# Graph stage: routing, ranks and scatters of a group one step later, the first gather directly behind the second sum

## The reference

```python
mask_punct = (punct_graph == 1) & (aug_adj != 1)      # both are adj here: always empty
mask_aug = aug_adj == 1
deg = jnp.maximum(masks.sum(axis=2), 1.0)[..., None]
def conv(x, w_rel, w_root, b):
    out = x @ w_root + b
    out = out + (masks^T @ x / deg) @ w_rel            # for each mask
h = elu(conv(layernorm(x), w_rel1, w_root1, b1))
x = x + elu(conv(h, w_rel2, w_root2, b2))
```

```python
z = layernorm(x)
rw = softmax(z @ Wr); topw, topi = top_k(rw, 2); topw = topw / sum(topw)
shared = gelu(z @ W1s + b1s) @ W2s + b2s
```

## Time and profile before

| what | value |
|---|---|
| median of 3 runs | 2830.13 us (2828.23 to 2833.62) |
| profiled execution, its own time | 2831.41 us |
| its span | 2829.7 us |
| PE busy | 2695.7 us (95%) |
| VectorE busy | 1966.7 us (70%) |
| ScalarE busy | 1461.8 us (52%) |
| GpSimd busy | 1503.5 us (53%) |

### The profile page before, as it was taken

How to read it: one execution, slowest core, us unless ns; L and a number is a source line. 1 busy time by engine, 2 the same in 40 slices (tenths; PEclk the granted TensorE clock), 3 DMA queues, 4 the chain that set the end, 5 groups by cost and what they waited for, 6 DMA issues and landing times. The chain is left out here.

```text
span 2829.7 us, 87893 instructions
## 1 busy us (share of the span) xinstructions
PE 2695.7 (95%) x28783; PEld 2136.2 (75%) x28784; DVE 1966.7 (70%) x6881; ACT 1461.8 (52%) x2930; POOL 1503.5 (53%) x2542
## 2 busy tenths in 40 slices
PE   8999999899989999999999989999998999999999
PEld 4666666599957777777777767777778999999988
DVE  5666666577778888888888858788874454545453
ACT  3444444455546666666666535455554444444444
POOL 5555555333234444444444427777761666666674
PEclk8999999999989999999999999999999999999999
DMA  1111111000000000000000011111232222222264
GB/s 52 30 37 30 36 31 46 3 0 0 0 1 0 0 0 0 0 0 0 0 0 0 1 35 58 57 56 56 85 115 61 75 76 81 75 80 77 71 195 147
DMA packets 158090, 118.01 MB, mean 42 GB/s; under 512 B 20150, under 2 KB 145593, under 8 KB 158010
## 3 DMA queue, kind: packets, MB, share of 16 engines
q1 hardware_dynamic: 140602, 81.02, 10.4%
q0 software_dynamic: 17408, 35.95, 3.8%
HBM read 68.36 MB, written 48.56 MB: 41 GB/s over the span
## 5 line engine op out<-in xcount | busy, mean ns | idle before, releaser
L2025 POOL DMA_INDIRECT token_y<-e_y,e_rows x288 | 294.7, 1023 | 78.8 <-issue 73.1
L2068 ACT ACTIVATE e_hidden<-e_ps,e_b1g 128x512 f32<-128x512 f32 x288 | 194.6, 688 | 258.4 <-PE e_ps L90 257.8
L833 POOL TENSOR_TENSOR s_sw<-s_expo,s_rsum 128x512 f32<-128x512 f32 x128 | 133.5, 1043 | 355.4 <-DVE s_rsum L1094 355.4
L1301 POOL DMA_INDIRECT sorted_z<-r_z,r_rows x256 | 264.8, 1034 | 66.6 <-issue 61.8
L2120 PE MATMUL e_ps<-expert_w,e_hidden 128*128 x2304 | 280.3, 275 | 0.0
L460 DVE TENSOR_REDUCE a_V<-a_ps_s 128x8 f32<-128x1024 f32 x128 | 156.9, 1226 | 176.8 <-PE a_ps_s L399 176.8
L2120 PEld LDWEIGHTS e_ps<-expert_w,e_hidden 128*128 128x128 f32 x2304 | 273.9, 192 | 6.3
L324 ACT ACTIVATE a_probT<-a_ps_st 128x1024 f32<-128x1024 f32 x128 | 131.2, 1025 | 203.3 <-PE a_ps_st L407 203.3
L399 PEld LDWEIGHTS a_ps_s<-a_nT 16*128 16x128 f32 x2048 | 136.2, 188 | 91.5 <-issue 55.6
L2197 DVE TENSOR_TENSOR e_biased<-e_ps,expert_b 128x512 f32<-128x512 f32 x72 | 49.8, 691 | 213.8 <-PE e_ps L2120 213.8
L399 PE MATMUL a_ps_s<-a_nT 16*128 16x128 f32 x2048 | 185.6, 299 | 11.1
(11 more groups left out here) (400 smaller groups left out, 8033.8 us busy)
## 6 DMA issues: line engine op xcount, KB each, us to landing
e_z<-sorted_z SPq DMA_DIRECT2D x72, 260.0 KB
c_y<-token_y SPq DMA_DIRECT2D x22, 512.0 KB, 4.1
X<-in_x_dram SPq DMA_DIRECT2D x32, 256.0 KB, 2.8
a_adj<-in_adj_dram SPq DMA_DIRECT2D x32, 256.0 KB, 2.8
g_adj<-in_adj_dram SPq DMA_DIRECT2D x32, 256.0 KB
out_dram<-X SPq DMA_DIRECT2D x32, 256.0 KB, 2.6
c_y_s<-token_y SPq DMA_DIRECT2D x10, 512.0 KB, 5.0
token_y<-e_y,e_rows POOLq DMA_INDIRECT x288
```

Of the source, the lines that this page charges most:

```text
L833: nc.gpsimd.tensor_tensor(sw[p][:, :, :], expo[p][:, :, :], rsum[p][:, 1, :].unsqueeze(2).to_broadcast([T, HEADS, C]), ALU.mult).then_inc( ...
L1301: nc.gpsimd.indirect_dma_start(sh.sorted_z, bass.IndirectOffsetOnAxis(ap=rows[own][:, e * GB + piece:e * GB + piece + 1], axis=0), zr[own] ...
L2025: nc.gpsimd.indirect_dma_start(sh.token_y, bass.IndirectOffsetOnAxis(ap=rows[p][:, b:b + 1], axis=0), y[p][:, b, :], None).then_inc(y_scat ...
L2068: nc.scalar.activation(hidden[p][:, c, :], ps_1[c % 2][:, :], ACT.Gelu, bias=b1g[p][:, c:c + 1]).then_inc(s["hidden_done"], 1)
```

## The change

The steps keep their number; the order within a step changes on four engines, and the routing of a group moves one step on.

- PE: the degrees of group t (not t+1) stand between the second gather and y1. Behind r1 stands the turning of zr of group t-2, then 2 (not 4) identity multiplications and the first gather. The logits of group t-2 stand behind the turning of z, then 10 identity multiplications (not 9 and 1). The ranks of group t-2 stand at the end of the step, behind r2.
- ScalarE: the copy of y1 is first in the step, ahead of the activations of group t-1; then come the copy of r1, the copy of zrT, and the activations of the first sum.
- VectorE: the first sum stands behind the second sum, the edges, the clipped degrees, z and the inverse degrees, and ahead of elu, residual and statistics of group t-1; h stands between the statistics and their aggregation; the routing of group t-2 stands behind that, ahead of zr of group t-1.
- GpSimd: the 8 scatters of a group are issued in one step. They wait for the second sum, the first sum, nothing, and the finished zr, in place of y2, r1 and the turned zr.
- In steps 31 to 33 the units of the shared branch are placed anew: shared(2) and (3) in step 32, shared(4) and (5) in step 33.

```diff
@@ GpSimd, step @@
+                own = (k + 1) % 4
+                late = 0 if known is None else max(known - groups, 0)
+                if live(known, 3, groups):
...
+                        pool.wait_ge(s["sum2_done"], t)
+                    nc.gpsimd.tensor_tensor(spare[:, k % 2:k % 2 + 1], ones[:, :], ones[:, :], ALU.add)\
+                      .then_inc(s["spare_done"], 1)
+                    scatter(own, 0)
...
+                        pause("second_paused", 4 + k % 2, t - 2, since(known, 5), s["sum1_done"], t + 1)
+                    scatter(own, 1)
                 if live(known, 1, groups):
                     pool.wait_ge(s["meanvar_done"], t)
...
+                    scatter(own, 2)
...
+                        pause("last_paused", 2 + k % 2, t - 2, since(known, 5), s["zr_done"], t)
+                    scatter(own, 3)
@@ PE, step, behind the second gather @@
+                if live(known, 0, groups):
+                    pe.wait_ge(s["edge_done"], t + 1)
...
+                    degrees(p)
@@ PE, behind r1 @@
+                if known == groups:
+                    shared(2)
+                if known == groups + 1:
+                    shared(4)
                 if live(known, 2, groups):
-
-                    pe.wait_ge(s["either_done"], t - 1)
...
+                    pe.wait_ge(s["zr_done"], t - 1)
...
+                        last = nc.tensor.transpose(ps_z[:, b * T:(b + 1) * T], zr[(k + 2) % 4][:, b, 0, 0:D], sh.ident[:, :])
+                    last.then_inc(s["zr_turned"], 1)
                 if live(known, 0, groups):
-                    keep_warm(4)
+                    keep_warm(2)
@@ PE, behind the turning of z @@
-                    keep_warm(9)
...
-                    degrees(q)
                 if known == groups:
-                    shared(2)
                     shared(3)
...
+                if known == groups + 1:
+                    shared(5)
+                if live(known, 2, groups):
+                    pe.wait_ge(s["zrT_done"], t - 1)
...
+                    last.then_inc(s["logits_done"], 1)
                 if live(known, 0, groups):
+                    keep_warm(10)
@@ VectorE, step @@
+                if live(known, 0, groups):
+                    dve.wait_ge(s["gathered1"], t + 1)
+                    dve.wait_ge(s["root1_copied"], t + 1)
+                    dve.wait_ge(s["rdeg_done"], t + 1)
+                    summed(sum1, ps_g1, k, s["sum1_done"])
                 if live(known, 1, groups):
                     dve.wait_ge(s["exp2_done"], t)
...
+                if known == groups - 1:
+                    f_split()
+                if live(known, 2, groups):
+                    dve.wait_ge(s["logits_done"], t - 1)
...
+                if known == groups:
+                    f_low(2)
+                    f_norm(3)
+                    f_add(0)
+                if known == groups + 1:
+                    f_low(4)
+                    f_norm(5)
+                    f_add(2)
```

More of the change, by code:

```diff
@@ L1324, in step @@
                 if live(known, 3, groups):
[L1325 to L1329, removed]
-                    else:
[L1331 to L1350, removed]
+                    if late:
+                        pause("first_paused", 6 + k % 2, t - 2, False, f["up_done"], (0, 13, 25)[late])
+                    scatter(own, 2)
+                    if known is not None and known >= groups:
+                        pause("last_paused", 2 + k % 2, t - 2, True, f["up_done"], (8, 15, 27)[late])
+                    else:
+                        pause("last_paused", 2 + k % 2, t - 2, since(known, 5), s["zr_done"], t)
+                    scatter(own, 3)
             run_rounds(pool, step, groups, LAG, PEEL)
@@ L1450, in step @@
                     last.then_inc(s["root1_done"], 1)
+                if known == groups:
+                    shared(2)
+                if known == groups + 1:
+                    shared(4)
                 if live(known, 2, groups):
[L1453 to L1458 removed]
+                    pe.wait_ge(s["zr_done"], t - 1)
+                    pe.wait_ge(s["zT_done"], t + 1 if known is None else min(known + 1, groups))
+                    if known is not None and known > groups:
+                        pe.wait_ge(s["zrT_done"], t - 2)
                     for b in range(GB):
[L1460 to L1462 removed]
+                        last = nc.tensor.transpose(ps_z[:, b * T:(b + 1) * T], zr[(k + 2) % 4][:, b, 0, 0:D], sh.ident[:, :])
+                    last.then_inc(s["zr_turned"], 1)
                 if live(known, 0, groups):
[L1464 removed]
+                    keep_warm(2)
                     pe.wait_ge(s["y1_done"], t + 1)
@@ L1503, in step @@
                     last.then_inc(s["h_turned"], 1)
[L1504 to L1515, removed]
                 if live(known, 0, groups):
@@ L1532, in step @@
                     last.then_inc(s["root2_done"], 1)
+                if live(known, 2, groups):
+                    pe.wait_ge(s["either_done"], t - 1)
+                    nc.tensor.matmul(ps_r[:, 1, :, :], before[:, :], either[:, :, :], start=True, stop=False)
+                    for b in range(GB - 1):
+                        nc.tensor.matmul(ps_r[:, 1, b + 1:GB, :], sh.ones_bf[:, :],
+                                         either[:, b:b + 1, :].to_broadcast([T, GB - 1 - b, EXPERTS]), start=False,
+                                         stop=(b == GB - 2))
+                    for b in range(GB):
+                        last = nc.tensor.matmul(ps_r[:, 2, 0, :], sh.ones_bf[:, :], either[:, b, :], start=(b == 0),
+                                                stop=(b == GB - 1))
+                    last.then_inc(s["ranked"], 1)
                 if known == groups - 1:
                     shared(1)
-                if known == groups:
-                    shared(5)
             run_rounds(pe, step, groups, LAG, PEEL)
@@ L1590, in step @@
[L1590 to L1599, removed]
@@ L1746, in step @@
                     last.then_inc(s["stats_done"], 1)
+                if live(known, 0, groups):
+                    dve.wait_ge(s["exp1_done"], t + 1)
+                    if since(known, 1):
+                        dve.wait_ge(s["h_turned"], t)
+                    nc.vector.scalar_tensor_tensor(out=h[:, :, :], in0=neg1[:, :, :], scalar=-1.0,
+                                                   in1=sum1[:, :, :], op0=ALU.add, op1=ALU.max)\
+                      .then_inc(s["h_done"], 1)
+                if live(known, 1, groups):
                     dve.wait_ge(s["stats_done"], t)
@@ new lines, in step @@
+                if live(known, 1, groups):
+                    dve.wait_ge(s["rstd_done"], t)
+                    if since(known, 5):
+                        dve.wait_ge(scattered[(k + 3) % 4], (r - 1 + (k + 3) // 4) * 2 * GB * 16)
+                    nc.vector.tensor_copy(sh.mean[:, bass.ds((t - 1) * GB, GB)], meanvar[q][:, :, 0])
+                    normalized(zr[(k + 3) % 4][:, :, 0, :], t - 1, meanvar[q], sh.rstd, s["zr_done"])
+                if known == groups:
+                    f_low(2)
+                    f_norm(3)
+                    f_add(0)
@@ L1844, in step @@
                 if known == groups - 1:
                     f_norm(0)
-                if known == groups:
-                    f_low(4)
-                    f_norm(5)
-                    f_add(2)
             run_rounds(dve, step, groups, LAG, PEEL)
```

216 lines of the change are left out of this document (101 added, 115 removed).

## The result

| kernel | median (range, runs) | ratio to the kernel before, 95% |
|---|---|---|
| before | 2831.88 us (2828.23 to 2834.39, 4) | |
| after | 2867.34 us (2852.87 to 2867.96, 4) | 1.0117 [1.0098, 1.0136] |

The account below looks back on a forecast made before the run. A graph-stage step was taken as bound by a closed chain of waits across engines, 13.69 us in the loop. From the profiled 2831.4: -6.0 steady steps, +9.8 last steps, -2 clock gives 2833.2; median 1.3 lower, 2832 us, range 2822 to 2841.

Parts of the forecast that it names:

- of the branch I leave 0.3 per pass: Graph-stage loop: its branch adds 0.3 us per four-step pass, 54.3 against 55.45 us before.
- the steady step: Graph stage, second gather to next second gather: 13.51 us; loop passes, step 1 and written-out steps together -6.0 us.
- the clock: TensorE's clock falls in the graph stage: two thirds of 7.3 us gone, one new fall of +3, together -2 us.
- the last steps: Steps 31 to 33: late f_norm and PE's waits for f_low lose +1.9 and +7.9, together +9.8 us.
- VectorE or GpSimd as the bound: Graph-stage steps: rows and scatters behind zr push the second sum, step 13.9 us, total 2844 us; chance 0.09.
- scatters that block the sums: Graph-stage steps: a scatter holds up VectorE's elu or X for 0.98 us per step, total 2860 us; chance 0.03.
- the 1.1 of zr: Step 32: VectorE's zr work, 1.1 us of PE's 4.0 us wait ahead of shared(4); step 33 has the wait without it.
- 1.1 in the sum: Last steps: one turning and one logits formerly hidden in step 31 now in the open, less the ranks, +1.1 us.
- the two nearer rivals: Steady steps: all clock falls go, step 0.2 shorter, 2821 us, chance 0.24; last steps: two falls, steady falls stay, 2840, 0.2.

Follow-up runs that it names:

- N = 0, 128: The changed kernel with no memsets, 2867.34 us, and with 128 one-element memsets ahead of VectorE's graph-stage code, 2864.78 us.
- N = 64: The changed kernel with 64 one-element memsets of unread columns ahead of VectorE's graph-stage code: 2850.28 us, one run.
- before with 104: The kernel before the change with 104 one-element memsets ahead of VectorE's graph-stage code: 2866.32 us, ratio 1.0133 to the kernel without them.

## Why the prediction was wrong

**The step that failed** is "of the branch I leave 0.3 per pass". It took the return of the loop to be what it was before, a constant of the kernel. It measured 7.3 us per return, 29.1 in all. At the first return, against the steady step of 13.54, 7.74 us are lost, and the rows divide them:

```profile
1828.27 0.68 DVE L1761 SCALAR_TENSOR_TENSOR g_h<-g_neg,g_sum 128x512 f32<-128x512 f32 x1
```

```profile
1827.73 4.43 PE L1363 MATMUL g_ps_h<-ident_bf 128*128 128x512 bf16 x10
1831.95 1.06 PE L1504 MATMUL g_ps_h<-ident,g_h 128*128 128x128 f32 x4
1833.70 1.16 PE L1510 MATMUL g_ps_y<-g_wrel,g_hT 128*128 128x128 f32 x8 [0.69 <-ACT g_hT L1613]
```

h starts 13.54 behind the second gather in place of 9.16: 4.4 us are left there of the wait of 5.44 for code. From h to y2 it is 5.43 in place of 2.07: 3.4 more come of the low clock, at which the ten identities take 4.43 in place of 2.32, so that PE is late for h. In the second return the two parts are 4.3 and 2.8. No rival had it. The trace of before could not have shown that it would come; its rows of 34 packets and of a wait for PE only showed that it was absent, and the change moved every instruction of VectorE's list ahead of and in the loop.

**With the placement taken out the forecast holds.** After with 24 memsets took 2833.73 beside 2832 forecast, and 1.001 [0.9991, 1.0028] of before: no change that can be told. That it comes so near is in part luck: the clock gave more than forecast and the last steps took more, as the next paragraphs show, and the two offset each other.

**The steady step** was right. Measured in after against the sum: second gather to first sum 5.83 (5.96), first sum to h 3.33 (3.39), h to y2 2.07 (1.43 + 0.65), y2 to the second gather 2.31 (2.08; the ranks' 0.2 stand here now, so both together are level). The rows of one step:

```profile
1801.19 1.14 PE L1431 MATMUL g_ps_g<-g_y,g_edge 128*128 128x128 f32 x8
...
1805.49 0.59 PE L1363 MATMUL g_ps_h<-ident_bf 128*128 128x512 bf16 x2
1805.92 1.05 PE L1477 MATMUL g_ps_g<-g_y,g_edge 128*128 128x128 f32 x8
...
1811.08 0.66 PE L1504 MATMUL g_ps_h<-ident,g_h 128*128 128x128 f32 x4 [0.44 <-DVE g_h L1761]
1812.42 1.16 PE L1510 MATMUL g_ps_y<-g_wrel,g_hT 128*128 128x128 f32 x8 [0.69 <-ACT g_hT L1613]
```

```profile
1807.02 1.13 DVE L1662 SCALAR_TENSOR_TENSOR g_sum<-g_ps_g,g_rdeg,g_sum 128x128 f32<-128x128 f32 x4 [1.49 <-PE g_ps_g L1477]
...
1810.35 0.67 DVE L1761 SCALAR_TENSOR_TENSOR g_h<-g_neg,g_sum 128x512 f32<-128x512 f32 x1
```

VectorE waits 1.49 ahead of the first sum (1.8 expected). The first pass, as yet without a return, takes 54.56 us (54.3 expected; 55.45 before). The wait of 13.6 us for rstd is gone but for one of 1.4. The scatters did not hold up VectorE: one at 1808.94 lies over the add to X, which takes 0.69 as in the earlier trace rows, and the elu ahead of it takes 0.68.

```profile
1808.78 0.69 DVE L1751 TENSOR_TENSOR X<-X,g_neg 128x512 f32 x1
```

```profile
1808.94 1.38 POOL L1301 DMA_INDIRECT sorted_z<-r_z,r_rows  x1 [0.15 <-issue]
```

So the rivals of VectorE or GpSimd as the bound, and of scatters that block the sums, are out.

**The last steps** lost as forecast, and more where I had no term. Step 31 took 17.19 (17.2 to 17.4). From the last second gather to shared(6) it was 41.99, +12.0 on the earlier trace rows, where +7.9 was forecast. PE in after:

```profile
2119.44 0.63 PE L1396 MATMUL g_ps_h<-ident,f_z 128*128 128x128 f32 x4 [3.02 <-DVE f_z L1690]
2119.90 1.83 PE L1431 MATMUL g_ps_g<-g_y,g_edge 128*128 128x128 f32 x8
2123.64 0.77 PE L88 MATMUL g_ps_r<-f_zTh,shared_w1h 128*128 128x512 f32 x1 [1.91 <-DVE f_zTl L1698]
...
2139.41 0.19 PE L1525 MATMUL r_ps_r<-r_either,r_before 128*128 128x32 bf16 x1 [2.20 <-DVE r_either L1799]
2141.11 0.79 PE L88 MATMUL g_ps_r<-f_zTh,shared_w1h 128*128 128x512 f32 x1 [1.34 <-DVE f_zTl L1698]
...
2161.29 0.21 PE L1525 MATMUL r_ps_r<-r_either,r_before 128*128 128x32 bf16 x1 [2.20 <-DVE r_either L1799]
2161.89 0.79 PE L88 MATMUL g_ps_r<-f_zTh,shared_w1h 128*128 128x512 f32 x1 [0.22 <-DVE f_zTl L1698]
```

Here two sums of the forecast are off by rounding: 4.0 less the 1.1 of zr is 2.9, not 2.8, and in the loop five passes of 54.34 against 55.45 are -5.55, not -5.7. The waits ahead of shared(4) are 2.20 + 1.34 = 3.5 (4.0), ahead of shared(6) 2.20 + 0.22 = 2.4 (2.8). The 1.91 ahead of shared(2) is no new wait; before has 1.73 there:

```profile
2101.42 0.47 PE L88 MATMUL g_ps_r<-f_zTh,shared_w1h 128*128 128x512 f32 x1 [1.73 <-DVE f_zTl L1697]
```

Behind each stall the clock falls: L88 takes 0.77 to 0.79 there, 0.47 in the earlier trace rows; the window has 0.82. The first half of shared(4), in after and in before:

```profile
2141.11:2147.64 6.53, 6.53 (x27) 5.84 (x27) 4.33 (x19) 3.26 (x5) 2.13 (x3) 0.53 0.07 23
```

```profile
2113.70:2117.31 3.61, 3.61 (x29) 3.30 (x28) 1.07 (x2) 2.76 (x5) 2.67 (x4) 1.00 0.17 55
```

Of the 12.0 the two waits are 6.0 and this half unit at the low clock 2.9; the other 3.1 are the pieces that now lie in the open (1.1 in the sum) and what the low clock costs around shared(2), which the rows do not part. The forecast had +9.8 and +3 for a new fall, 12.8 together; step 31 and the way to shared(6) in after gave 1.9 + 12.0 = 13.9.

**The clock.** In the steady steps of after with 24 memsets no fall is left; two thirds had been forecast to go. So the term was -7.3 and some +3 in the last steps, -4.3 in place of -2. In after itself the falls of the returns stand on top. Each of the two nearer rivals came true by half: the clock gain was whole, but the step was no shorter than worked out; the stalls of the last steps took the clock down, but the steady steps did not keep their falls.

The difference of the two profiled executions: the stage begins 2.0 later, its steps to the last second gather take 19.5 more (29.1 at the returns and 1.9 in step 31, less the loop's steps, step 1 and the old falls), and the rest of the kernel 15.1 more (12.0 to shared(6), and 3.1 behind it). One of the four runs of after took 2852.87; its trace was not taken, and what it left out is open.

## What to carry to other kernels

A hardware loop whose body is long on one engine can stay loaded at one place of that engine's code and not at another; any edit ahead of it or in it may tip it. In the profile look for an "issue" wait of some us on the first instruction of the body at each return, and for more packets on the engine's instruction queue; a pad of a few idle instructions separates this from the edit's own worth, and writing the loop out removes it. Fill an engine only where it waits anyway (and even there the filler stands in the way once the clock is low, as at the returns), and put what the last iterations need ahead of what only they postpone.

## What the runs showed of the hardware

- The instructions on q14 come in blocks of 8192 bytes (0.44 MB in 54 packets; those on q8, the other such queue, in blocks twice as large, 0.74 MB in 45), and right behind a return one follows the other after 2.5 us (1817.3, 1819.8, 1822.3).
- A VectorE body of 346 instructions stays over five passes in some places (1 block on the whole queue from 1835 to 2060) and is read again in others, with five blocks per return; the wait at the return is then 5.3 to 6.0 us (N = 0, 128), 3.0 to 3.3 (N = 64), or 2.9 to 3.2 and then 1.4 to 1.5 more ahead of the edges (before with 104), and 0.5 or less where it stays.
- 128 memsets gave the times of none, so the pattern looks to repeat with 128 instructions. If the places between those measured are like them, the bad range is at least 64 long and the good one at least 34 (6 to 40). Where exactly the edges lie stays open. All of it fits a body that stays where it touches three blocks of 128 and not where it touches four; that is an argument from nine places, and no run shows what the memory holds.
- Read in order, blocks cost nothing that the steps show (13.11 each, 24 blocks on q14 in 400 us).
